# A decoder layer on one core: the next batch's context taken apart into 32 slots among the present batch's stages

## The chip, the core and the metric

The kernel runs as one program on one NeuronCore of a Trainium2 chip. The metric is the time of one execution on the device in microseconds (us), the median of several runs. All arithmetic is float32, except the attention scores, whose float32 operands are split into three bfloat16 parts.

## What is computed

For each of 8 batches: a self-attention block, a cross-attention block with an MLP, and a feed-forward block whose operands are rounded to FP4 values in blocks of 16. In short:

```python
x = x + attn(layernorm(x))               # x: (8, 512, 256), 16 heads of 16, relative keys and values
Q = layernorm(x); C = ctx                # ctx: (8, 1601, 256)
q, k, v = LN(Q) @ wq, LN(C) @ wk, LN(C) @ wv            # 16 heads of 64
out = (l2norm(q) @ l2norm(k).T) @ v @ wo                # no softmax
y = Q + out + bo
x = x + y + gelu(LN(y) @ w1 + b1) @ w2 + b2
x = x + fp4(silu(fp4(z) @ wg.T) * (fp4(z) @ wu.T)) @ wd.T       # z = layernorm(x)
```

Cross-attention has no softmax, so keys and values enter only through one matrix. With kn the normed keys and Cn the normed context, the kernel forms G = kn.T @ Cn per pair of heads, then the block diagonal of G @ wv, then M = that @ wo (1024 x 256), and needs only qn @ M for the present batch. M depends on the context alone, not on x.

## The kernel before

One hardware loop runs over the 8 batches (`Fori(0, NB)` on every engine; b is the batch). PE is TensorE, DVE is VectorE, ACT is ScalarE, POOL is GpSimd, SP issues most DMAs. The order on each engine is the order of the program text; engines meet only at semaphores, and an instruction that waits holds all that is behind it on its engine. Within a batch the stages follow one another:

1. **Projection of x.** Normed x is transposed; K, Q and V are projected; `R` (queries against the 41 relative keys) comes from four tiles of `bdk` matmuls. K and Q are split into three bfloat16 parts.
2. **Context.** 13 tiles of 128 rows of the context (the last has 65). A tile is loaded, normed (`norm_stats`, `norm_apply`), transposed (`t_ctx`), projected to 1024 key columns (`k_ctx`), squared and summed by heads, scaled by a root that POOL computes (`norm_root`, a power function, line 367), and added to G (`g_ctx`), which fills PSUM banks 0 to 3. Beside it run the transfers that prepare attention: SP stores the band part of R and the bfloat16 parts to DRAM scratch and reads the parts back, rearranged, as `Kp`, `Kfar` and `Qp`; POOL builds the far edges of the bias (`Eb`, 8 pieces of 512 KB, two buffers, line 679) in `far_edge`, and ACT's own DMA queue stores them (`store_edge`, line 832).
3. **G to M** (G is transposed, multiplied by wv, masked, multiplied by wo).
4. **Attention**, four tiles of 128 queries by 16 heads: scores on PE, bias and minimum on DVE (line 1115), exponential on ACT (line 862), transposes and the product with V on PE. SP loads bias windows and stores probabilities.
5. **Band, output projection, norm**: `transpose_band`, `weigh_band`, `combine`, `project`, layer norm.
6. **Cross-attention**: `project_q`, roots on POOL, transposes and the product with M; then the norm of y.
7. **MLP** (two products, 8 blocks of 128 hidden units).
8. **FFN**: two quantisations of 256-row halves (`quant_scale`, `quant_abs`, `quant_count`, `quant_finish`), `gate_up` and `down` for four tiles with a quantisation each. POOL's share of a tile is `quant_divide` (line 405) and `quant_finish` (lines 434 and 439). The norm of the next batch's x runs behind the last tile.

Before the loop, the FFN weights are quantised and transposed; this takes the first 124 us.

## Time and profile before

| | |
|---|---|
| median of 3 runs | 3678.69 us (3668.11 to 3689.46) |
| the profiled execution | 3670.19 us |
| its span, from the first to the last instruction | 3668.3 us |
| PE busy | 2691.3 us, 73% |
| DVE busy | 1985.8 us, 54% |
| ACT busy | 1195.6 us, 33% |
| POOL busy | 1153.9 us, 31% |
| mean granted TensorE clock | 0.897 of full speed |
| moved by DMA | 259.07 MB |

The busy shares are averages over stages with different limits, and no engine is near its whole span. The stages repeat every 440 us or so, and they are told apart by asking for the busy time in windows of one batch. The second batch, from 576.8 to 1017.2 us, is the one read below.

### The profile page before, as it was taken

How to read it: one execution, taken by the hardware profiler on the slowest of the kernel's cores; microseconds unless marked ns; L12 is line 12 of the kernel's file. 1: busy time of each engine (PE TensorE's matmuls, PEld its weight loads, DVE VectorE, ACT ScalarE, POOL GpSimd, SP SyncE). 2: the span in 40 equal slices, each digit the busy share in tenths (PEclk: the TensorE clock that was granted, in tenths of full speed). 3: DMA queues.
4: the chain of work that ended last, by engine and by line, in shares of the span. 5: the costliest groups of instructions: out<-in, count | busy, mean ns of one | idle time of the engine just before them, and what ended most of it. 6: DMA issues, size and time to landing. Idle time of an engine off the chain costs nothing.

```text
span 3668.3 us, 48646 instructions
## 1 busy us (share of the span) xinstructions
PE 2691.3 (73%) x14836; PEld 1813.0 (49%) x14884; DVE 1985.8 (54%) x4001; ACT 1195.6 (33%) x1925; POOL 1153.9 (31%) x812
## 2 busy tenths in 40 slices
PE   0487777877787776867768777687777867787776
PEld 0255544554455544555445545355544554455544
DVE  5646465463754537545375554646455464654537
ACT  1226222271233612344123432225223271233611
POOL 1352223422243123521235222362223522244122
PEclk9999988998899987998879989799888998899987
DMA  6365004650056400663008520364104650056400
GB/s 195 34 127 135 20 6 53 123 145 7 2 85 124 112 6 13 100 128 82 6 18 127 120 58 6 32 137 126 28 6 48 128 141 6 8 76 127 118 6 6
DMA packets 503886, 259.07 MB, mean 71 GB/s; under 512 B 213166, under 2 KB 501702, under 8 KB 502598
## 3 DMA queue, kind: packets, MB, share of 16 engines
q1 hardware_dynamic: 436982, 221.53, 31.0%
q10 hardware_dynamic: 66560, 33.56, 4.0%
q8 instruction: 142, 2.33, 0.2%
q14 instruction: 202, 1.65, 0.2%
HBM read 129.67 MB, written 125.35 MB: 70 GB/s over the span
## 4 chain that ended last, share of the span: by engine, by line
PE 50%; DVE 19%; issue 10%; ACT 8%; POOL 4%; DMA 4%; ACTq 1%; DVEq 1%; POOLq 0%; another core or an unknown queue 0%
PE PS L1273 44%; PE PS L1276 7%; DMA bias_scr<-M 4%; DVE arena L422 3%; ACT arena L862 2%; ACT arena L869 2%; DVE arena L427 2%; DVE arena L419 2%; POOL rn L367 1%; POOL rstd L367 1%; POOL arena L439 1%; DVE PS L1115 1%; DVE arena L424 1%; DVE arena L1072 1%; DVE arena L429 1%
## 5 line engine op out<-in xcount | busy, mean ns | idle before, releaser
L1276 PE MATMUL PS<-ident,arena 128*128 128x128 f32 (+1 forms) x3356 | 571.3, 299 | 628.5 <-POOL arena L439 289.8
L1276 PEld LDWEIGHTS PS<-ident,arena 128*128 128x128 f32 (+1 forms) x3356 | 410.9, 152 | 822.4 <-POOL arena L439 313.0
L1273 PE MATMUL PS<-arena 128*17 128x128 f32 (+5 forms) x6624 | 729.5, 318 | 106.6 <-ACT arena L869 60.1
L1273 PEld LDWEIGHTS PS<-arena 128*17 128x17 f32 (+2 forms) x6656 | 510.2, 126 | 214.1 <-ACT arena L869 68.1
L367 POOL TENSOR_TENSOR rn<-rn,mhalf 128x16 f32<-128x16 f32 (+1 forms) x136 | 412.9, 3036 | 475.0 <-DVE rn L1065 264.7
L1115 DVE CUSTOM_DVE_ANT_0 PS<-PS,arena 128x512 f32<-128x512 f32 x512 | 343.2, 712 | 97.0 <-PE PS L1273 68.9
L1273 PE MATMUL PS<-cwk,arena 128*128 128x512 f32 (+1 forms) x832 | 376.1, 595 | 23.7 <-ACT arena L801 21.0
L862 ACT ACTIVATE arena<-PS,nmax 128x512 f32<-128x512 f32 x512 | 352.1, 690 | 74.3 <-DVE nmax L1115 65.5
L716 POOL TENSOR_TENSOR arena<-arena,mass_mask 128x512 f32<-128x512 f32 x128 | 163.3, 1276 | 571.9 <-ACT arena L862 571.9
L367 POOL TENSOR_TENSOR rstd<-rstd,mhalf 128x1 f32<-128x1 f32 (+3 forms) x153 | 104.0, 680 | 719.6 <-DVE rstd L380 300.9
L1063 DVE TENSOR_REDUCE ss<-arena 128x16 f32<-128x1024 f32 (+1 forms) x104 | 126.9, 1220 | 285.1 <-ACT arena L807 285.1
L869 ACT ACTIVATE arena<-PS 128x512 f32<-128x512 f32 x384 | 228.9, 597 | 120.5 <-PE PS L1273 116.7
L801 ACT ACTIVATE arena<-PS 128x1024 f32<-128x1024 f32 (+1 forms) x104 | 106.4, 1023 | 483.0 <-PE PS L1273 473.4
L1273 PEld LDWEIGHTS PS<-cwk,arena 128*128 128x128 f32 (+1 forms) x832 | 152.7, 186 | 190.0 <-issue 180.8
L1273 PE MATMUL PS<-wdT,arena 128*128 128x256 f32 (+1 forms) x384 | 165.1, 603 | 32.1 <-ACT arena L943 32.1
L439 POOL TENSOR_TENSOR arena<-arena 128x704 f32<-128x704 f32 (+2 forms) x58 | 87.1, 1501 | 322.2 <-DVE arena L429 322.2
L1273 PE MATMUL PS<-cwq,arena 128*128 128x512 f32 x256 | 160.9, 793 | 35.1 <-DVE arena L1217 27.9
L1122 DVE COPY arena<-PS 128x512 f32<-128x512 f32 x128 | 88.4, 691 | 166.2 <-PE PS L1273 166.2
L679 POOL TENSOR_TENSOR M<-tail_mask,arena 128x1024 f32<-128x1024 f32 x64 | 122.1, 1908 | 112.7 <-DMA bias_scr<-M 112.7
L1273 PEld LDWEIGHTS PS<-wdT,arena 128*128 128x128 f32 (+1 forms) x384 | 112.0, 309 | 82.1 <-ACT arena L943 44.8
L1273 PE MATMUL PS<-M,arena 128*128 128x256 f32 x512 | 118.1, 384 | 40.2 <-issue 19.5
L1072 DVE TENSOR_TENSOR arena<-arena,rn 128x1024 f32<-128x1024 f32 (+1 forms) x104 | 126.6, 1218 | 22.9 <-POOL rn L367 22.9
(163 smaller groups left out, 3763.2 us busy)
## 6 DMA issues: line engine op xcount, KB each, us to landing
arena<-bias_scr SPq DMA_DIRECT2D x128, 336.0 KB, 3.2
prob_scr<-arena SPq DMA_DIRECT2D x128, 336.0 KB, 3.7
bias_scr<-M ACTq DMA_DIRECT2D x64, 512.0 KB, 4.8
q_scr<-arena SPq DMA_DIRECT2D x128, 128.0 KB
arena<-k_scr SPq DMA_DIRECT2D x64, 256.0 KB, 10.9
arena<-q_scr SPq DMA_DIRECT2D x128, 128.0 KB, 3.2
arena<-in_ctx SPq DMA_DIRECT2D x96, 128.0 KB, 2.5
arena<-far_scr SPq DMA_DIRECT2D x64, 182.0 KB, 17.0
```

The source lines that it names most:

```text
L367: pool.tensor_tensor(x, x, mhalf[0:x.shape[0], 0:x.shape[1]], ALU.pow).then_inc(done, 1)
L422: st(eng.scalar_tensor_tensor(c, a, m, c, ALU.is_gt, ALU.add))
L439: eng.tensor_tensor(X, qc[0:parts, p, 0:n], qh[0:parts, p, 0:n], ALU.mult).then_inc(quant_out, 1)
L679: pool.tensor_tensor(Eb[:, k, :, :], tail_mask[:].unsqueeze(1).broadcast_to([128, HC, 128]), bcast(Rb[:, t, k * HC:(k + 1) * HC, BAND], 12 ...
L716: pool.tensor_tensor(prod[:], P[:, (g % 2) * HG:(g % 2 + 1) * HG, t * 128 + BAND:t * 128 + BAND + 128], mass_mask[:].unsqueeze(1).broadcas ...
L862: act.activation(P[:, (g % 2) * HG + j, PAD:PAD + S], bank(j), ACT.Exp, bias=nmax[:, j:j + 1], scale=-1.0).then_inc(probs_ready, 1)
L869: act.activation(PTs[:, j, :], bank(TBANKS[j]), ACT.Copy).then_inc(pt_copied[0], 1)
L1063: st(dve.tensor_reduce(ss[0:n, p, :], csq[0:n].rearrange("p (h c) -> p h c", c=XD), AX.X, ALU.add))
L1072: dve.tensor_tensor(k, k, bcast(rn[0:n, q % 2, :], XD), ALU.mult).then_inc(cs_ready, cinc(i))
L1115: dve.tensor_tensor_reduce(out=bank(j), in0=bank(j), in1=Wz[:, at:at + S], scale=-0.25, scalar=BIG, op0=ALU.add, op1=ALU.min, accum_out=nm ...
L1273: return pe.matmul(o, l, r, start=start, stop=stop, **kw)
L1276: return pe.transpose(o, i, ident[0:i.shape[0], 0:i.shape[0]])
```

## The change

The context part of a batch leaves its place in the batch. For batch 0 it runs before the loop; inside the loop every engine works on the present batch b and on the context, the G-to-M products and the projection of x of batch b + 1.

- **Slots.** The context is cut into 26 half tiles (two passes of 13 tiles over 512 key columns each), run as 32 slots numbered -6 to 25, each slot with one piece on each engine. `SLOTS_AT` says behind which piece of the present batch each slot stands, the same on every engine: -6 to 2 behind the four band tiles, 3 to 6 behind the output projections, 7 to 11 behind the norm, 12 to 23 among the cross-attention tiles, 24 and 25 at the norm of y. The MLP products have none.
- **PSUM.** The present batch keeps banks 0 to 3 from the band stage to the MLP, the slots have banks 4 to 7. Banks that were double buffers in the band and cross stages become single: the band transposes (banks 0 and 1 for every tile), `project_q` (banks 2 and 3), the projected keys of a slot (bank 6).
- **G to M** of b + 1 stands between the four `second` products of the MLP; the projection of x of b + 1 follows them, ahead of the FFN.
- **The transfers that prepare attention** (`prepare`) stand, for b + 1, behind the present batch's attention on SP, in this order: R, the parts, a wait for all of them, Kp, Qp, Kfar, and then the far edges, now 16 pieces of 256 KB in two buffers, issued by SP and no longer by ACT. SP's stores of the output come after all of them.
- **POOL** builds the 16 far edges four at a time inside the FFN loop, behind each tile's `quant_divide` and the previous tile's `quant_finish`; each waits for the store of the piece before it in its buffer, and the first waits for `part2_ready`.
- At the start of an iteration SP waits until the output is stored, then loads the first bias windows.
- The loop still runs 8 times, each with the next batch's context; the ninth context is a batch of zeros appended to the input.

```diff
+PASSES = 2
+CSTEPS = PASSES * CT
+HALF = INNER // PASSES
+MP = NM // PASSES
+FIRST = -6
+MBANKS = (6, 7, 2, 3)
+LOADS = ((0, 1), (1, 4), (4, 8), (8, 12), (12, 13))
+EQ = HG * 128
+SLOTS_AT = {("band", 0): (-6, -5, -4), ("band", 1): (-3, -2), ("band", 2): (-1, 0), ("band", 3): (1, 2),
+            ("wo", 0): (3,), ("wo", 1): (4,), ("wo", 2): (5,), ("wo", 3): (6,), "ln": (7, 8, 9, 10, 11),
+            ("x", -1): (12, 13, 14), ("x", 0): (15, 16, 17), ("x", 1): (18, 19), ("x", 2): (20, 21), ("x", 3): (22, 23),
+            "yn": (24, 25), ("h", 1): (), ("h", 3): (), ("h", 5): (), ("h", 7): ()}
...
+            def prepare(nb):
+                for t in range(T):
+                    sp.wait_ge(r_act, 2 * (T * nb + t + 1) + 1)
                     sp.sem_inc(waits_alone, 1)
                     sp.dma_start(bias_scr[t].rearrange("h (p r) -> p h r", r=SKEW)[:, :, 0:BAND],
                                  Rb[:, t, :, 0:BAND]).then_inc(bias_stored, 16)
-
-                def store_keys(i):
-                    if i == 0:
-                        sp.wait_ge(part1_ready, 2 * (b + 1) + 1)
-                        sp.sem_inc(waits_alone, 1)
-                        sp.wait_ge(part2_ready, 2 * (b + 1) + 1)
-                        sp.sem_inc(waits_alone, 1)
-                        sp.wait_ge(far_ready, 3 * (b + 1) + 1)
-                        sp.sem_inc(waits_alone, 1)
+                sp.wait_ge(part1_ready, 2 * (nb + 1) + 1)
+                sp.sem_inc(waits_alone, 1)
+                sp.wait_ge(part2_ready, 2 * (nb + 1) + 1)
+                sp.sem_inc(waits_alone, 1)
+                sp.wait_ge(far_ready, 3 * (nb + 1) + 1)
+                sp.sem_inc(waits_alone, 1)
+                for i in range(PARTS):
                     sp.dma_start(k_scr[i].rearrange("(c r) s -> r c s", c=2), kparts[:, i, :, :]).then_inc(parts_stored, 16)
                     sp.dma_start(far_scr[i].rearrange("(c r) s -> r c s", c=2), farparts[:, i, :, :]).then_inc(parts_stored, 16)
-
-                def store_q(slot):
+                for slot, part in enumerate(SLOTS_Q):
                     for c in range(2):
                         sp.dma_start(q_scr[slot * HD:(slot + 1) * HD, c * HC:(c + 1) * HC, :].rearrange("d h s -> h d s"),
-                                     qparts[:, SLOTS_Q[slot], c, :]).then_inc(parts_stored, 16)
-
-                def more_ctx(i, q):
-                    if i < PARTS:
-                        store_keys(i)
-                    elif i < PARTS + 4:
-                        store_q(2 * (i - PARTS))
-                        store_q(2 * (i - PARTS) + 1)
-                    if exists(i + CSLOTS):
-                        load_ctx(i + CSLOTS)
-                ctx_unrolled(more_ctx)
-                sp.wait_ge(parts_stored, 16 * STORES * (b + 1) + 1)
+                                     qparts[:, part, c, :]).then_inc(parts_stored, 16)
+                sp.wait_ge(parts_stored, 16 * STORES * (nb + 1) + 1)
                 sp.sem_inc(waits_alone, 1)
-
-                def load_q(t, g):
-                    sp.dma_start(Qp[:, g * HG:(g + 1) * HG, :],
-                                 q_scr[:, g * HG:(g + 1) * HG, t * 128:(t + 1) * 128]).then_inc(q_loaded[g], 16)
-
                 for slot, part in enumerate(SLOTS_K):
                     sp.dma_start(Kp[slot * HD:(slot + 1) * HD, :, :], k_scr[part].rearrange("(h d) s -> d h s", d=HD))\
                         .then_inc(k_loaded, 16)
+                for g in range(NG):
+                    load_q(nb, 0, g)
                 for slot, part in enumerate(SLOTS_K):
                     sp.dma_start(Kfar[slot * HD:(slot + 1) * HD, :, :], far_scr[part].rearrange("(h d) s -> d h s", d=HD))\
                         .then_inc(k_loaded, 16)
-                for g in range(NG):
-                    load_q(0, g)
-
+                for t in range(T):
+                    for g in range(NG):
+                        sp.wait_ge(eb_ready, NG * (T * nb + t) + g + 2)
+                        sp.sem_inc(waits_alone, 1)
+                        sp.dma_start(bias_scr[t, g * HG:(g + 1) * HG].rearrange("h (p r) -> p h r", r=SKEW)[:, :, BAND:BAND + 128],
+                                     Eb[:, g % 2, :, :]).then_inc(eb_stored[g % 2], 16)
...
+                load_ctx(b + 1)
+                load_x(b + 1)
+                prepare(b + 1)
...
+            def far_edge(nb, t, g):
+                if t == 0 and g == 0:
+                    pool.wait_ge(r_act, 2 * T * (nb + 1) + 1)
+                    pool.sem_inc(waits_alone, 1)
+                    pool.wait_ge(part2_ready, 2 * (nb + 1) + 1)
+                    pool.sem_inc(waits_alone, 1)
+                pool.wait_ge(eb_stored[g % 2], 16 * (2 * (T * nb + t) + g // 2) + 1)
+                pool.sem_inc(waits_alone, 1)
+                pool.tensor_tensor(Eb[:, g % 2, :, :], tail_mask[:].unsqueeze(1).broadcast_to([128, HG, 128]),
+                                   bcast(Rb[:, t, g * HG:(g + 1) * HG, BAND], 128), ALU.mult).then_inc(eb_ready, 1)
...
-                        quant_divide(pool, gs[:, t, :], t % 2, 128, FF)
+                        quant_divide(pool, gs[:, t % 2, :], t % 2, 128, FF)
                     if t:
-                        if t >= 3:
-                            pool.wait_ge(ht_psum, T * b + t - 1)
-                            pool.sem_inc(waits_alone, 1)
-                        quant_finish(pool, st, hq[:, (t - 1) % 2, :], (t - 1) % 2, 128, FF, NQ0 + b * QPB + NXQ + t - 1)
+                        quant_finish(pool, st, qc[:, (t - 1) % 2, :], (t - 1) % 2, 128, FF, NQ0 + b * QPB + NXQ + t - 1)
+                    if t < T:
+                        for g in range(NG):
+                            far_edge(b + 1, t, g)
...
+            def slot(nb, s):
+                j = s + 3
+                if 0 <= j < CSTEPS:
+                    i, p, n = j % CT, j // CT, crows(j % CT)
+                    pe.wait_ge(ct_ready, ctile(nb, i))
+                    pe.wait_ge(kc_ready, cstep(nb, j - 1))
                     for c in range(2):
...
+                        ins = mm(bank(6, parts=n), cnT[:, i, c, 0:n], cwk[:, c, p * HALF:(p + 1) * HALF], c == 0, c == 1)
+                    ins.then_inc(ck_psum, 1)
+                i = s + 4
+                if 0 <= i < CT:
+                    n = crows(i)
+                    pe.wait_ge(caff_ready, ctile(nb, i))
+                    pe.wait_ge(ct_ready, ctile(nb, i - 1))
+                    for c in range(2):
+                        ins = tr(bank(7, c * 128, c * 128 + n), cn[0:n, i, c * 128:(c + 1) * 128])
+                    ins.then_inc(ct_psum, 1)
+                if 0 <= s < CSTEPS:
+                    i, n = s % CT, crows(s % CT)
+                    if i == 0:
+                        if s:
+                            pe.wait_ge(g_act, PASSES * nb + 2)
+                            pe.wait_ge(g_dve, PASSES * nb + 2)
+                        for k in (4, 5):
+                            mm(bank(k), zeros[:, 0:128], zeros[:], True, True, skip_group_check=True)
+                    pe.wait_ge(cs_ready, cstep(nb, s))
+                    for m in range(MP):
+                        ins = mm(bank(4 + m // 2, (m % 2) * E, (m % 2 + 1) * E), kns[0:n, s % 4, m * 128:(m + 1) * 128], cn[0:n, i, :],
+                                 False, True, skip_group_check=True)
+                    ins.then_inc(cg_done, 1)
...
+                evac_g(b + 1, 1)
+                add_x2(0)
+                copy_gt(b + 1)
+                add_x2(1)
+                mask_kv(b + 1)
+                add_x2(2)
+                copy_m(b + 1)
+                add_x2(3)
+                norm_x2(0)
+                norm_x(b + 1)
+                quant_count(dve, st, 0, 128, XQ * E, NQ0 + b * QPB)
+                norm_x2(1)
+                first_rests(b + 1)
+                quant_count(dve, st, 1, 128, XQ * E, NQ0 + b * QPB + 1)
+                second_rests(b + 1)
...
+                    if t == 0:
+                        last_parts(b + 1)
...
+                second(0)
+                transpose_g(b + 1)
+                second(1)
+                key_values(b + 1)
+                second(2)
+                context_out(b + 1)
+                second(3)
+                project_x(b + 1)
```

On DVE a slot holds, in this order: the statistics of tile s + 6, the sum of squares of step s + 2 (8 heads), the two passes that norm tile s + 5, the scaling of step s + 1. On POOL it holds the roots for the first two, on ACT the copy of the keys of step s + 3, the copy of the transposed tile s + 4 and the square of step s + 3.

## Rows read from the trace of the kernel before

**Rows 1.** Windows: length; busy PE, PEld, DVE, ACT, POOL; clock; DMA share; GB/s.

```profile
0.00:124.00 124.00, 9.10 (x42) 6.52 (x43) 82.72 (x154) 13.42 (x21) 28.14 (x27) 1.00 0.50 144
...
576.80:598.00 21.20, 14.49 (x40) 8.11 (x40) 7.82 (x18) 7.68 (x11) 2.44 (x5) 0.86 0.13 40
598.00:718.40 120.40, 102.82 (x349) 65.82 (x350) 57.11 (x103) 31.55 (x43) 62.41 (x35) 0.93 0.79 116
718.40:732.00 13.60, 9.79 (x70) 8.93 (x72) 5.43 (x9) 3.45 (x6) 3.27 (x4) 1.00 0.17 52
732.00:829.00 97.00, 68.85 (x886) 51.65 (x887) 62.25 (x162) 68.52 (x121) 20.45 (x16) 0.96 0.53 138
829.00:843.00 14.00, 13.58 (x100) 11.19 (x100) 5.68 (x18) 2.32 (x5) 0.00 (x0) 1.00 0.00 1
...
848.00:856.50 8.50, 2.50 (x8) 1.26 (x8) 6.15 (x18) 0.78 (x1) 4.86 (x6) 0.71 0.00 1
...
829.00:926.30 97.30, 75.69 (x293) 46.71 (x293) 35.32 (x78) 17.68 (x26) 23.31 (x19) 0.88 0.02 6
926.30:1017.20 90.90, 61.55 (x208) 42.73 (x208) 69.30 (x113) 17.01 (x31) 28.75 (x20) 0.79 0.02 6
...
926.30:962.10 35.80, 27.40 (x104) 20.02 (x104) 23.22 (x49) 5.00 (x8) 6.54 (x6) 0.86 0.00 1
```

**Rows 2.** PE in order of time, one tile of the context: start, length, instructions.

```profile
630.79 3.60 PE L1273 MATMUL PS<-cwk,arena 128*128 128x512 f32 x8
634.22 0.38 PE L1276 MATMUL PS<-ident,arena 128*128 128x128 f32 x2
634.44 3.62 PE L1273 MATMUL PS<-arena 128*128 128x256 f32 x16
637.90 3.60 PE L1273 MATMUL PS<-cwk,arena 128*128 128x512 f32 x8
```

**Rows 3.** DVE in order of time, one tile of the context.

```profile
636.70 1.22 DVE L1063 TENSOR_REDUCE ss<-arena 128x16 f32<-128x1024 f32 x1 [2.67 <-ACT arena L807]
...
638.04 0.48 DVE L1026 SCALAR_TENSOR_TENSOR arena<-arena,mv,rows 128x256 f32<-128x256 f32 x1
...
639.07 1.22 DVE L1072 TENSOR_TENSOR arena<-arena,rn 128x1024 f32<-128x1024 f32 x1
640.20 0.42 DVE L1015 BATCH_NORM_STATS2 bnst<-arena 128x6 f32<-128x256 f32 x1
```

**Rows 4.** SP's issues in order of time, from the context to attention.

```profile
598.15 9.93 SPq L529 DMA_DIRECT2D bias_scr<-arena  x4
...
645.83 2.44 SPq L545 DMA_DIRECT2D q_scr<-arena  x4
...
667.31 3.77 SPq L565 DMA_DIRECT2D arena<-k_scr  x8
671.13 15.54 SPq L568 DMA_DIRECT2D arena<-far_scr  x8
686.71 9.79 SPq L561 DMA_DIRECT2D arena<-q_scr  x4
```

**Rows 5.** The page, part 6: issues, KB each, median us to landing.

```profile
arena<-bias_scr SPq DMA_DIRECT2D x128, 336.0 KB, 3.2
...
bias_scr<-M ACTq DMA_DIRECT2D x64, 512.0 KB, 4.8
```

**Rows 6.** Waits, 598 to 718.4: who waited for whom, total, times, longest.

```profile
POOL M L679 <- DMA bias_scr<-M: 14.9, 2, 14.2
```

**Rows 7.** POOL and DVE in order of time, FFN tiles and the end.

```profile
978.32 1.44 POOL L405 TENSOR_TENSOR arena<-arena,qrc 128x704 f32<-128x704 f32 x1 [1.88 <-DVE qrc L397]
...
990.47 1.43 POOL L405 TENSOR_TENSOR arena<-arena,qrc 128x704 f32<-128x704 f32 x1 [1.88 <-DVE qrc L397]
...
1008.46 1.67 POOL L439 TENSOR_TENSOR arena<-arena 128x704 f32<-128x704 f32 x1 [6.10 <-DVE arena L429]
...
1016.78 0.42 DVE L1264 TENSOR_TENSOR arena<-arena,PS 128x256 f32<-128x256 f32 x1 [3.16 <-PE PS L1273]
```

931 lines of the change are left out of this document (471 added, 460 removed).

## The prediction, made before the changed kernel was run

> **What bounds the kernel now.** I read part 1 of the page first, the busy times in the table above: PE has 73% of the span and no other engine more than 54%, so nothing is full all the time and stages must be taken one by one. The windows of one batch [rows 1] give them. The reader is to see four kinds. In the context (120.4 us) PE is busy for 102.8; a full tile takes 3.60 of keys, 0.38 of transposes (partly overlapped) and 3.62 of G, one every 7.11 us [rows 2], so 13 tiles are 92.4 us of pure PE and 28 us are lost, half of it in one wait of POOL for a far-edge store, 14.9 us [rows 6]. Attention (97.0 us) mixes ACT, DVE and PE and isn't touched. From the band to the end of the first MLP product (829.0 to 926.3, 97.3 us) PE is busy for 75.7 at a granted clock of 0.88: chains of small steps on DVE, ACT and POOL. Behind it (90.9 us) DVE's quantisation sets the pace, 12.15 us a tile as POOL's steps repeat [rows 7]. DMA is heavy beside the context (share 0.79) and nearly nil from 829 to 1017 (0.02) [rows 1]: all that prepares attention hides under the context.
>
> **The gap to be won, and what is paid first.** In the loop the stages ahead of attention (21.2 + 120.4 + 13.6 = 155.2 us) leave their place. But the change runs one context pass, projection and preparation before the loop and still eight in it. So the first attention starts at:
>
> - start-up 124 [rows 1], loads of x and context behind it 3 (a 336 KB window lands in 3.2 [rows 5]);
> - 32 slots: the first three hold only norm pieces (about 2 us each), the next ten have norm pieces on DVE (3.8 each, below), nineteen are PE's 3.55: 6 + 38 + 67, and 8 of latency: 119;
> - G to M 14 [rows 1]; norm and projection of x to the last bfloat16 part 34 (the 21.2 window, 5 for the norm, 8 for R's last tiles and the parts);
> - the stores of R (four issues took 9.93 [rows 4]; 12 beyond the parts' end) and of the parts (17, below), with no work to hide them, 29; Kp, Qp and Kfar 25; 16 far edges 38; first window 4.
>
> Sum 390 us to the first bias step. The end adds no window (-4) and the launch lies 2 outside the span (3670.19 against 3668.3). So time = 388 + 8P, P being the new period, and **the kernel is only faster if P is under 410.3** ((3670.2 - 388) / 8), where a batch now takes 440.4. That bar rests on no guess about the overlap beyond the 390.
>
> **Front half, band to first MLP product (X).** Floor: PE's own work is 75.7 at clock 0.88, 66.6 at full clock, and the slots add 92.4, together 159. Slot by slot it comes out longer, since each slot also holds DVE pieces in DVE's program order: half of 1.22 for the sum, half of 1.22 for the scaling, and for the first 13 slots two of 0.48 and 0.42 plus small ones [rows 3]; with its self-waits (0.15 us steps between them) 3.7 us a full slot.
>
> - Band, now 14: nine slots. DVE 5.7 of its own, four light slots at 2.1, five full at 3.7: 33. The band transposes now have one bank, so tile t+1's wait for an ACT copy that stands behind tile t-1's slots: about 4 us at each of two tiles. 41.
> - Output projection: four slots at 3.7 and 1 to 1.5 of DVE's own each: 21.
> - Norm: five slots of PE 3.55 = 17.8, but slot 8's scaling stands behind the whole norm chain on DVE, 7 of the window's 8.5 us [rows 1]: PE stalls 5.5; transposes and copies 2.2. 25.5.
> - Cross: four `project_q` at 3.6 for eight records and four M products at 3.6 [rows 2], transposes 4.2, twelve slots (the last without keys) 41, evacuation of G at slot 13, 2. 76.
> - Norm of y 7.3 (its chain is as long as now; PE's last two slots hide under it), first MLP product 14.9 at full clock.
>
> X = 185 against 97.3. Bounds 159 (PE without a stall) and 200.
>
> **Back half, end of the first MLP product to the last output (T).** Now 90.9 [rows 1]. The first tile's quantiser scale stands at 35.8 [rows 1]. Put in front of it: G-to-M matmuls between the second MLP products, 9.8 of PE; the norm of x, 5; the projection, 21.2; and a serial piece: `quant_abs` of the second half waits on ACT behind the copies of R, and `quant_count` behind it, 7. That is 79; `last_parts`, two of 1.2 and one of 0.9, end at 82. From there:
>
> - SP stores 6 + 16 pieces. 4 of the q kind cost 2.44 to issue [rows 4], so 16 take 9.8, the keys' 3, landing 4: 17. At 99.
> - Kp, Kfar and Qp: before, their issue took from 667.3 to 696.5, 29.2 us [rows 4], with two 512 KB edge stores beside them. Alone I take 25; bounds 18 and 30. At 124.
> - Only now is the first far edge stored, since SP issues in order; 256 KB land in about 3.5 (4.8 for 512 KB, 3.2 for a 336 KB window [rows 5]). At 127.5.
> - POOL has stood since 82 + 2: the third far edge needs the first one's buffer. Behind it on POOL are `quant_divide(1)` and `quant_finish(0)`, for which ACT, DVE and PE's `down(0)` wait. DVE counts tile 0 and scales tile 1 meanwhile, then it is out of work too.
> - Then three tiles at 12.15 or, by the edges, two buffer cycles of 4.8 and 5 of POOL's own, about as much: 36.5; and from the last `quant_finish` (1008.46) to the last output (1017.2) 8.7 [rows 7].
>
> T = 127.5 + 1.5 + 36.5 + 8.7 = 174. **The stall is 36 us of it**: without it the tiles would follow from 79 on, 79 + 4 x 12.15 + 8.7, and 2 for the edges' own time, 138. Its bounds are 25 and 45.
>
> A rule of the Trainium skill bears on the edges' move from ACT's issue to SP's (page DMA: Bandwidth & Descriptors, section Issuing engines are not separate DMA queues): DMAs from any engine share 16 DMA engines, and several issuers save only issue time. Taken so, the move costs 16 issues at 0.4, 6 us over the batch, and T would be about 145. The trace agrees on the sharing (14.9 us of waiting even from ACT's own queue [rows 6]); the rest of the stall comes from program order and buffers, which the rule doesn't cover.
>
> Between iterations, now hidden under G to M: output store and the wait for it 2.5, window issue and landing 4 [rows 5]: 6.5. Attention 97.0.
>
> P = 97 + 185 + 174 + 6.5 = **462.5**, 22 more than now: all 155 us taken out come back, 88 in X, 83 in T, 6.5 between. Time = 388 + 8 x 462.5 = **4088 us**, 11% slower, set against the profiled 3670.19; the median shown lies 8.5 higher, which is within what I can't resolve.
>
> **The rivals.**
>
> 1. *No stall of POOL.* The edges land early, as when the loads drain faster than their issue shows. For it: DMA is idle when `prepare` starts, and loads have no context loads beside them. Against: SP's order. P = 426.5, time 3800.
> 2. *PE sets the front half.* DVE's and ACT's order costs nothing, X = 159 + 5. For it: once full, the context took 7.11 us a tile, no more than its own matmuls [rows 2]. Against: each slot is followed by a piece of the batch with a serial chain. P = 441.5, time 3920.
> 3. *Faster: engines, not chains, bind everywhere.* PE never idles from the band to the MLP (159), because its clock stays at full and each slot covers a wait, and the same full packing behind it leaves DVE alone: 69.3 busy now [rows 1], some 18 more for what moves there, and starts and ends, T = 120. P = 97 + 159 + 120 + 6.5 = 382.5, time 3448. It decides as soon as the two halves together lose under 28 us to waits (P under 410.3). Against: both halves have named waits of over 25.
> 4. *Worse:* a full slot costs 4.3 on DVE and the edges queue behind each other's landings (6 a cycle): X 195, T 185, P 483, 4250.
>
> **Chances.** Forecast 0.60, rival 1 0.13, rival 2 0.12, rival 3 0.08, rival 4 0.07. From no change, measurement here can tell about 0.5%. Faster 0.08, same 0.02 (between rivals 1 and 3), slower 0.90. Range: the forecast's own is 4000 to 4180 (each of X, T off by 6); taking in rivals 1 and 2, 3800 to 4190.
>
> **What would show it.** First bias step at 390; period 462; POOL idle for some 35 to 43 us in each FFN, released by a DMA of the far edges, with DVE idle in the same stretch; DMA share above 1 there; band to MLP 185 with the granted clock at 1.0 and PE idle some 14%. Wrong if the FFN shows no POOL wait over 15 us, or if the first bias step comes before 350.

## The result and the profile after

The changed kernel takes 4299.28 us (4297.52 to 4303.79), the kernel before 3676.12 on the same chip: 1.169 of its time, interval 1.166 to 1.173. Direction and mechanism came out as forecast. The size did not: 4088 was forecast, 4190 was the upper end of the range.

The page's part 1 and two groups of its part 5 (busy and mean of one, then the idle time of the engine just before them and what ended it):

```profile
PE 2823.7 (66%) x15346; PEld 1925.3 (45%) x15346; DVE 2101.9 (49%) x4415; ACT 1302.0 (30%) x2282; POOL 1351.9 (31%) x1041
...
L679 POOL TENSOR_TENSOR arena<-tail_mask,arena 128x512 f32<-128x512 f32 x144 | 177.5, 1246 | 596.6 <-DMA bias_scr<-arena 561.6
...
L404 DVE TENSOR_REDUCE am<-arena 128x44 f32<-128x704 f32 (+2 forms) x58 | 46.6, 803 | 433.4 <-POOL arena L454 420.4
```

PE, DVE and ACT are emptier than before (66, 49 and 30% for 73, 54 and 33%), POOL is at its 31%. POOL alone stands 561.6 us in front of its far-edge products, for the stores of earlier ones, and of the 433.4 us that DVE stands idle before its scalings 420.4 are for POOL's quantiser. The second batch by stages, in the columns of [rows 1]: attention; band; output projection; norm; cross attention; norm of y; first MLP product; from there to the first row tile's scaling; the row tiles:

```profile
871.10:968.60 97.50, 70.82 (x878) 53.01 (x878) 62.05 (x161) 68.30 (x120) 20.41 (x16) 0.92 0.55 138
968.60:1018.40 49.80, 40.66 (x163) 27.13 (x164) 25.78 (x76) 10.34 (x23) 13.71 (x14) 0.79 0.11 33
1018.40:1038.00 19.60, 19.35 (x82) 13.59 (x81) 15.57 (x41) 6.77 (x16) 9.63 (x9) 1.00 0.01 1
1038.00:1062.70 24.70, 20.75 (x73) 13.15 (x71) 13.47 (x37) 7.24 (x13) 12.22 (x8) 0.93 0.00 1
1062.70:1139.00 76.30, 72.78 (x270) 49.10 (x271) 32.62 (x59) 20.14 (x31) 35.07 (x20) 0.98 0.00 1
1139.00:1146.70 7.70, 5.29 (x25) 3.65 (x24) 5.44 (x14) 0.84 (x2) 4.94 (x6) 0.98 0.00 1
1146.70:1162.90 16.20, 15.51 (x32) 6.64 (x32) 0.55 (x1) 6.67 (x10) 2.17 (x4) 0.90 0.11 33
1162.90:1242.00 79.10, 58.53 (x234) 41.65 (x235) 39.34 (x75) 23.57 (x39) 12.59 (x10) 0.85 0.36 17
1242.00:1352.80 110.80, 32.78 (x96) 21.52 (x94) 48.09 (x52) 9.47 (x20) 42.02 (x32) 0.61 0.60 110
```

X is rows two to seven, 194.3 us (forecast 185), T the last two, 189.9 (174). Nearly all of X's excess is in the band: 49.8 instead of 41, at a granted clock of 0.79 (1.3 more are in the first MLP product, and the output projection gives 1.4 back). All of T's is in the last row, where PE is busy for a third of the time.

What T waits for, on POOL in order of time (batch before that one). A far edge is L679, the divide of a row tile L420:

```profile
746.91 2.13 POOL L420 TENSOR_TENSOR arena<-arena,qrc 128x704 f32<-128x704 f32 x1 [12.92 <-DVE qrc L412]
750.51 2.36 POOL L679 TENSOR_TENSOR arena<-tail_mask,arena 128x512 f32<-128x512 f32 x2 [1.46 <-DVE arena L1116]
805.71 1.05 POOL L679 TENSOR_TENSOR arena<-tail_mask,arena 128x512 f32<-128x512 f32 x1 [52.84 <-DMA bias_scr<-arena]
...
807.98 1.38 POOL L420 TENSOR_TENSOR arena<-arena,qrc 128x704 f32<-128x704 f32 x1
```

and on SP, whose issues run in program order:

```profile
754.25 10.34 SPq L553 DMA_DIRECT2D q_scr<-arena  x16
768.19 3.77 SPq L558 DMA_DIRECT2D arena<-k_scr  x8
772.00 12.90 SPq L533 DMA_DIRECT2D arena<-q_scr  x4
784.94 6.67 SPq L563 DMA_DIRECT2D arena<-far_scr  x8
791.81 16.66 SPq L569 DMA_DIRECT2D bias_scr<-arena  x4
```

The first two edges are built by 752.9 and their first store is issued at 791.8, behind 17 us of stores and 23.5 us of load issues. It lands just before 805.7, 13.9 us after its issue. The loads issued ahead of it are still landing: the eight of Kfar do so at 793.2 to 803.9, the store at 805.5. In windows from the first load's issue to that landing (the last two columns are the DMA share and GB/s):

```profile
768.00:784.00 16.00, 0.00 (x0) 0.00 (x0) 0.00 (x0) 0.00 (x0) 0.00 (x0) 0.50 1.07 113
784.00:792.00 8.00, 0.00 (x0) 0.00 (x0) 0.00 (x0) 0.00 (x0) 0.00 (x0) 0.50 1.28 139
792.00:806.00 14.00, 0.00 (x0) 0.00 (x0) 0.00 (x0) 0.00 (x0) 0.29 (x1) 0.50 1.09 123
```

For 52.84 us POOL does nothing, and from 768 us on no engine does. Every batch has one such wait (52.2 to 53.1 us), and 8 of them and the prologue's 67.3 make most of the 561.6. The DMA share above 1 is the one that the prediction gave as a sign.

The tables below give four stretches of a batch, read from the order of time and averaged over a run's eight batches (the border over seven): scores (first to last bias step), front (from there to the last sum of the cross attention), back (from there to the last output) and border (to the next first bias step).

### The profile page after: what moved, and what is told of

Read it like the earlier page. It is cut to its first block, busy times and chain, and to the rows that moved or that the text cites. A ratio compares the mean times of both kernels' runs of the same rounds, so it can differ in the third digit from the quotient of the medians.

```text
span 4301.3 us, 51796 instructions
## 1 busy us (share of the span) xinstructions
PE 2823.7 (66%) x15346; PEld 1925.3 (45%) x15346; DVE 2101.9 (49%) x4415; ACT 1302.0 (30%) x2282; POOL 1351.9 (31%) x1041
## 4 chain that ended last, share of the span: by engine, by line
PE 50%; DVE 15%; issue 9%; SPq 8%; ACT 6%; DMA 5%; POOL 3%; ACTq 1%; DVEq 0%; POOLq 0%
PE PS L1341 44%; PE PS L1344 7%; DMA bias_scr<-arena 3%; SPq L533 3%; SPq L553 2%; ACT arena L885 2%; DVE arena L442 2%; ACT arena L878 2%; SPq L563 1%; DVE arena L437 1%; POOL rstd L382 1%; DMA q_scr<-arena 1%; DVE PS L1144 1%; DVE arena L439 1%; POOL arena L454 1%
## 5 line engine op out<-in xcount | busy, mean ns | idle before, releaser
L1341 PE MATMUL PS<-arena 128*17 128x128 f32 (+6 forms) x6864 | 809.9, 320 | 140.8 <-ACT arena L878 71.1
L1341 PEld LDWEIGHTS PS<-arena 128*17 128x17 f32 (+3 forms) x6864 | 553.7, 128 | 311.5 <-issue 93.7
L1341 PE MATMUL PS<-cwk,arena 128*128 128x512 f32 (+1 forms) x936 | 476.7, 634 | 14.5 <-ACT arena L798 14.5
L382 POOL TENSOR_TENSOR crn<-crn,mhalf 128x8 f32<-128x8 f32 (+1 forms) x234 | 419.8, 1800 | 177.7 <-DVE crn L1060 176.8
L679 POOL TENSOR_TENSOR arena<-tail_mask,arena 128x512 f32<-128x512 f32 x144 | 177.5, 1246 | 596.6 <-DMA bias_scr<-arena 561.6
L793 ACT ACTIVATE arena<-PS 128x512 f32<-128x512 f32 (+1 forms) x234 | 139.7, 597 | 699.1 <-PE PS L1341 699.1
L404 DVE TENSOR_REDUCE am<-arena 128x44 f32<-128x704 f32 (+2 forms) x58 | 46.6, 803 | 433.4 <-POOL arena L454 420.4
L1058 DVE TENSOR_REDUCE css<-arena 128x8 f32<-128x512 f32 (+1 forms) x234 | 159.6, 682 | 94.1 <-ACT arena L803 92.3
L382 POOL TENSOR_TENSOR crs<-crs,mhalf 128x1 f32<-128x1 f32 (+1 forms) x117 | 69.9, 598 | 406.8 <-DVE crs L1051 398.8
L1079 DVE TENSOR_TENSOR arena<-arena,crn 128x512 f32<-128x512 f32 (+1 forms) x234 | 160.4, 685 | 74.9 <-POOL crn L382 74.0
L382 POOL TENSOR_TENSOR rn<-rn,mhalf 128x16 f32<-128x16 f32 x32 | 93.0, 2905 | 290.2 <-DVE rn L1245 290.2
```

The lines of the kernel that those rows point to most:

```text
L382: pool.tensor_tensor(x, x, mhalf[0:x.shape[0], 0:x.shape[1]], ALU.pow).then_inc(done, 1)
L679: pool.tensor_tensor(Eb[:, g % 2, :, :], tail_mask[:].unsqueeze(1).broadcast_to([128, HG, 128]), bcast(Rb[:, t, g * HG:(g + 1) * HG, BAND] ...
L793: act.activation(kns[0:n, j % 4, :], bank(6, parts=n), ACT.Copy).then_inc(kc_ready, 1)
L1058: st(dve.tensor_reduce(css[0:n, j % 2, :], csq[0:n, j % 2, :].rearrange("p (h c) -> p h c", c=XD), AX.X, ALU.add))
L1079: dve.tensor_tensor(k, k, bcast(crn[0:n, j % 2, :], XD), ALU.mult).then_inc(cs_ready, 1)
L1341: return pe.matmul(o, l, r, start=start, stop=stop, **kw)
```

## The experiments

All are edits of the changed kernel unless the text says otherwise. Where no range or interval stands beside a time, it is that of one run, good to some 0.3%.

### 1. The edges taken out of the loop, and their stores alone

POOL doesn't build the edges, and SP's stores of them go too, by the lines of the second diff:

```diff
-                    if t < T:
-                        for g in range(NG):
-                            far_edge(b + 1, t, g)
```

> Left out: the far edges of the bias are neither built nor stored for any batch but the first (16 GpSimd products and 16 stores of each next batch). Measured so far in the changed kernel: period 490.9 us, of which 189.9 from the end of the first MLP product to the last output, with one GpSimd wait of 52.8 and row tiles of 14.4 instead of 12.15. Theory A (the edges cost both, the wait for their stores and the slower tiles beside their building): the stage falls to about 126 to 130, the period to 427 to 431, the time to 3800 to 3835 us. Rival B (the wait alone goes; the tiles stay at 14.4 for another reason): period 438, time about 3885. Rival C (SyncE's serial stores and loads of the keys end the batch anyway): the period stays over 465 and the time over 4100.

For the second run the loop above stays, and SP leaves its stores out (POOL then waits for no store, and ACT waits once a batch until the edges are built):

```diff
             def prepare(nb):
...
+                if nb is not 0:
+                    return
                 for t in range(T):
                     for g in range(NG):
                         sp.wait_ge(eb_ready, NG * (T * nb + t) + g + 2)
```

> Left out: the stores of the far edges of every batch but the first; they are still built, by the same 16 GpSimd products in the same places, which wait for nothing. Against the run without any edges the difference is the price of building them beside VectorE. Theory A (GpSimd's tensor products slow VectorE and lie in the row tiles' chain): some 9 to 15 us a batch more than the run without edges, time about 3880 to 3950. Rival B (building is free, the whole loss is the wait for the stores): within 3 us a batch of it, within 25 us in all.

Measured: 3850.1 and 3899.9 us. Against 4299.3 that is 56.1 us a batch for the edges, 49.9 of it for their stores and 6.2 for the building. The first lies between its theories A and B: the tiles do speed up, but not all four. POOL's divides without edges:

```profile
1180.94 2.14 POOL L420 TENSOR_TENSOR arena<-arena,qrc 128x704 f32<-128x704 f32 x1 [12.92 <-DVE qrc L412]
1187.74 1.44 POOL L420 TENSOR_TENSOR arena<-arena,qrc 128x704 f32<-128x704 f32 x1 [4.67 <-DVE qrc L412]
...
1199.88 1.44 POOL L420 TENSOR_TENSOR arena<-arena,qrc 128x704 f32<-128x704 f32 x1 [1.88 <-DVE qrc L412]
...
1214.39 1.44 POOL L420 TENSOR_TENSOR arena<-arena,qrc 128x704 f32<-128x704 f32 x1 [4.24 <-DVE qrc L412]
```

They follow each other by 6.8, 12.14 and 14.5 us: 12.15 [rows 7] holds for the middle one, and the last waits for `gate_up(3)`, which the change put behind `down(0)`: PE starts it at 1205.7, right behind that product, and the divide follows at 1214.4. The second run falls in its theory A's time and below its 9 to 15 us a batch.

### 2. The stores in another order

With four buffers instead of two, in the room of the queries and keys; the four stores of a query tile at each of four places in SP's order:

```diff
+                store_edges(nb, 0)
                 for slot, part in enumerate(SLOTS_Q):
...
+                store_edges(nb, 1)
                 for slot, part in enumerate(SLOTS_K):
                     sp.dma_start(Kp[slot * HD:(slot + 1) * HD, :, :], ...
...
```

> Nothing left out. Four edge buffers instead of two (in the room of the queries and keys, free once their parts are taken), and SyncE issues the four edge stores of a query tile in between: tile 0 before the stores of the query parts, tile 1 before the loads of the keys, tile 2 before those of the far keys, tile 3 behind them. Theory A (the loss is the edge stores standing behind 17 us of stores and 23.5 us of loads in SyncE's queue): GpSimd hardly waits, period 438 to 450, time 3885 to 3985. Rival B (the edges' own transfers are the limit, 16 of them at 2.2 us each, wherever they stand): their 35 us are on the path at least in part, period 460 to 475, time 4065 to 4180.

Measured: 3978.6 us, 40.1 a batch better, within A's time and far from B's (the first bias step also comes 14 us earlier, 368.4 for 382.3, so the batches themselves gain 38.8). "Hardly waits" was too much: what is left is on POOL, whose last edges wait for stores that stand behind the loads of Kp and Qp:

```profile
1242.80 1.05 POOL L684 TENSOR_TENSOR arena<-tail_mask,arena 128x512 f32<-128x512 f32 x1 [10.15 <-DMA bias_scr<-arena]
```

So I went one step further: buffers in the room of the normed x, half the edges built ahead of the row tiles, all stored ahead of the loads, which wait until the stores have landed.

```diff
-        Eb = carve(2 * EQ, (2 * EQ,), ot_at)...
+        Eb = carve(NG * EQ, (NG * EQ,), 2 * PARTS * 512)...
...
                         add_bo(b + 1)
+                for t in range(2):
+                    for g in range(NG):
+                        far_edge(b + 1, t, g)
                 for t in range(T + 1):
...
```

> Nothing left out. Four edge buffers lie in the room of the normed x (free after the value projection), so that building no longer waits for the last parts of the queries and keys: GpSimd builds query tiles 0 and 1 before the first row tile of the FFN, tiles 2 and 3 behind the first two scalings, and SyncE stores them before the key loads. Known: the changed kernel's period is 490.9 us, 450.8 with the stores in between (10 us of waits for a landing left in the last row tile), 440.9 with edges built and not stored, 434.8 without edges. Theory A (once no store stands behind a load, what is left is the building, half of it in GpSimd's idle time before the first row tile): period 436 to 441, time 3855 to 3905. Rival B (16 stores of 256 KB cost their 35 us wherever they stand, now before the part stores): the loads of the keys come late instead and attention starts late, period 450 to 460, time 3970 to 4060.

Measured: 3937.6 us, 45.2 a batch better, between the two theories. The wait has moved ahead of the first divide (1185.8), for the stores of the first four edges. These stand behind no load, but behind SP's four stores of R (320 KB each), the last of which lands at 1179.2; the first edge's store is issued at 1166.4 and lands at 1180.4, 14.0 us later, as behind the loads:

```profile
1164.62 4.73 POOL L682 TENSOR_TENSOR arena<-tail_mask,arena 128x512 f32<-128x512 f32 x4
1180.58 1.05 POOL L682 TENSOR_TENSOR arena<-tail_mask,arena 128x512 f32<-128x512 f32 x1 [11.24 <-DMA bias_scr<-arena]
```

```
us a batch             scores  front  back   border
changed kernel           88.1  180.5  212.1   10.1
no edges                 89.1  180.5  157.0    7.5
edges built, unstored    88.7  180.3  164.6    6.6
stores in between        89.1  180.0  171.0   11.9
edges early              88.3  179.9  168.0   11.0
```

So the place in SP's order cost 40 to 45 us a batch, and rival B of both runs, that 16 stores cost their 35 us wherever they stand, is out. What wasn't tried is the issuer: the edges' stores back on ACT's queue, as in the kernel before. The front does not answer to the edges at all; it is the other question.

### 3. Where the context steps stand

```diff
-            ("wo", 0): (3,), ("wo", 1): (4,), ("wo", 2): (5,), ("wo", 3): (6,), "ln": (7, 8, 9, 10, 11),
+            ("wo", 0): (), ("wo", 1): (), ("wo", 2): (), ("wo", 3): (), "ln": tuple(range(-6, 26)),
...
```

> Nothing left out. All 32 context steps of the next batch stand in one place, behind the first norm, instead of being dealt out over band, output projection, norm and cross attention (and TensorE waits for all attention rows before the first output projection). Theory A (dealing them out hides the short waits of the present batch's own steps): the stretch from the band to the first MLP product grows from 194.3 to about 209, the period to 506, the time to about 4420. Rival B (TensorE is the bound of the stretch either way, the slots only fill what they take): within 4 us a batch, time 4270 to 4330. Rival C (the slots in between stall TensorE more than they fill, as the 4.25 us wait in the band shows): 5 to 10 us a batch faster, time about 4220 to 4260.

```diff
-SLOTS_AT = {("band", 0): (-6, -5, -4), ("band", 1): (-3, -2), ("band", 2): (-1, 0), ("band", 3): (1, 2),
+SLOTS_AT = {("band", 0): (), ("band", 1): (-6, -5, -4), ("band", 2): (-3, -2), ("band", 3): (-1, 0),
...
```

> Nothing left out. The first context steps of the next batch stand behind the second band tile instead of the first, the following ones one place later each, up to the norm. In the changed kernel TensorE idles 4.25 us in the band for the first normed context tile (974 us) and the granted clock is 0.5 to 0.8 for the next 25 us, where the kernel before has 1.0 in its band. Theory A (the first step comes before its tile is loaded and normed, and the band then runs at the lower clock; that is the 9 us by which the stretch from band to first MLP product was longer than forecast): the band's clock is 1.0, the stretch shortens by 4 to 9 us, time 4225 to 4270. Rival B (the idle time and the low clock only move to where the steps now start, or to the norm): within 2 us a batch, time 4280 to 4315. Rival C (fewer steps hidden in the band: 3 steps more in the norm): 2 to 5 us a batch slower, up to 4340.

```diff
-SLOTS_AT = {("band", 0): (-6, -5, -4), ("band", 1): (-3, -2), ("band", 2): (-1, 0), ("band", 3): (1, 2),
+SLOTS_AT = {("band", 0): (), ("band", 1): (), ("band", 2): (), ("band", 3): (),
...
+            "yn": (18, 19), ("h", 1): (20, 21), ("h", 3): (22, 23), ("h", 5): (24,), ("h", 7): (25,)}
```

> Nothing left out. The steps are dealt out behind the output projections, the norm, the cross attention and the MLP products (8 of the 32 among the last), none in the band. Theory A (TensorE has no gap among the MLP products, so 6 context tiles cost their full 5.4 us there, and the band runs without them at full clock): the stretch from the band to the last MLP product stays within 4 us of the changed kernel's, time 4265 to 4335. Rival B (it matters little where the steps stand as long as they are dealt out, but the band's low clock goes): 4 to 9 us a batch faster, 4225 to 4265. Rival C (the band and MLP places are worse for the waits of the present batch): 5 us a batch slower or more, over 4340.

Measured: 4408.5, 4305.0 and 4179.4 us. (In the first and the third PE also waits for all attention rows before the first output projection.) All in one place costs 13.7 us a batch (A): that is what the dealing out is worth. One tile later changes nothing (B). With none in the band and six among the MLP products (my expectations say eight; the two before them stand in the norm of y, as two did) it is **15.0 us a batch faster**, beyond all three theories I wrote.

```
us a batch             scores  front  back   border
all in one place         87.7  193.7  213.0    9.9
one tile later           88.3  179.8  212.7   10.0
none in the band         88.0  150.0  227.6    9.8
```

30.5 us less in front, 15.5 more behind (the MLP is in that stretch). Two windows of that kernel (fourth batch), the band up to DVE's last combine, and norm of y with the first MLP product:

```profile
1909.40:1925.40 16.00, 14.67 (x106) 11.78 (x104) 6.15 (x20) 3.05 (x7) 0.00 (x0) 0.96 0.34 104
...
2052.60:2089.30 36.70, 35.80 (x119) 21.59 (x119) 12.82 (x31) 13.65 (x20) 17.85 (x15) 1.00 0.05 15
```

Between the same marks the band shrinks from 44.7, with seven of its nine steps, to 16.0. Norm of y and first MLP product, with eight steps in place of two, grow from 23.3 to 36.7, by 13.4 where PE's busy time grows by 15.6 (20.2 to 35.8): a step there costs no more than its matmuls, since the first ones also fill the waits of the norm. In the band seven steps take 28.7 us for 20.8 more of PE's busy time. What part of this is a lower clock and what part waits is the next question.

### 4. The wait in the band and the clock

PE in the band of the changed kernel, second batch, and the windows just there:

```profile
971.53 1.28 PE L1341 MATMUL PS<-bdv,arena 128*128 128x68 f32 x10
977.05 0.68 PE L1344 MATMUL PS<-ident,arena 128*128 128x128 f32 x2 [4.25 <-DVE arena L1072]
978.78 1.33 PE L1344 MATMUL PS<-ident,arena 128*128 128x128 f32 x5 [1.04 <-ACT arena L909]
...
983.22 2.34 PE L1341 MATMUL PS<-bdv,arena 128*128 128x68 f32 x10
```

```profile
974.60:980.60 6.00, 2.51 (x9) 1.70 (x10) 3.77 (x14) 0.87 (x2) 2.12 (x3) 0.59 0.01 4
980.60:986.60 6.00, 6.00 (x22) 4.78 (x22) 1.17 (x5) 0.00 (x0) 0.00 (x0) 0.50 0.00 0
```

PE waits 4.25 us for the first normed context tile. Not for its load, which was issued at 967.5: on DVE the tile's first norm piece stands behind the band's own combine, which waits for PE's band products,

```profile
972.84 0.26 DVE L1189 RECIPROCAL rl<-PS 128x16 f32<-128x16 f32 x1 [2.33 <-PE PS L1341]
...
973.94 0.42 DVE L1046 BATCH_NORM_STATS2 cbn<-arena 128x6 f32<-128x256 f32 x1
...
976.44 0.48 DVE L1072 SCALAR_TENSOR_TENSOR arena<-arena,crs,rows 128x256 f32<-128x256 f32 x1 [0.16 <-DVE arena L1068]
```

so that PE's transposes of that tile wait for a chain that starts at the product PE did just before them. With the steps one tile later the same wait stands one tile later, which is why that won nothing:

```profile
985.54 0.69 PE L1344 MATMUL PS<-ident,arena 128*128 128x128 f32 x2 [4.26 <-DVE arena L1072]
```

After it the granted clock is 0.5, the lower of its two levels (1.2 of 2.4 GHz), and ten records that took 1.28 us at 971.5 take 2.34 at 983.2. Two kernels fill the wait with products of zeros, whose results nobody reads (the second diff is against the first):

```diff
                     weigh_band(t)
+                    if t == 0:
+                        for _ in range(14):
+                            mm(bank(7), zeros[:, 0:128], zeros[:], True, True, skip_group_check=True)
                     slots(("band", t))
```

> Nothing left out. In the changed kernel TensorE waits 4.25 us in the band for the first normed context tile, and the granted clock is 0.5 to 0.8 for 25 us from there on. Here 14 products of zeros (0.3 us each) stand in that place. Theory A (the low clock follows from the idle time, and the low clock is why the band took 49.8 us where 41 was forecast): the band's clock is near 1.0, 6 to 9 us a batch shorter, time 4225 to 4250. Rival B (the clock falls whatever TensorE does there, or the band is held by the waits between the engines and not by its clock): within 2 us a batch, 4285 to 4315.

```diff
-                        for _ in range(14):
-                            mm(bank(7), zeros[:, 0:128], zeros[:], True, True, skip_group_check=True)
+                        for _ in range(20):
+                            mm(bank(4), zeros[:, 0:128], zeros[:], True, True, skip_group_check=True)
                     slots(("band", t))
+                    if t < 2:
+                        for _ in range(5):
+                            mm(bank(4), zeros[:, 0:128], zeros[:], True, True, skip_group_check=True)
```

> Nothing left out. As the run with 14 products of zeros in the band's wait (4271.1 us; there 1.2 us of idle time were left and the clock fell all the same in most batches), now with 20 in that place and 5 in each of the two next waits. Theory A (the idle time decides on the clock): the clock stays at 1.0 through the band in nearly all batches, which makes the stretch from the last score to the cross attention's end 172 to 173 us instead of 180.7 in nearly all of them, time 4230 to 4245. Rival B (the two good batches were chance, the band is held by the waits between engines): 4265 to 4290.

Measured: 4271.1 us, then 4244.0. With 14 products the front is 174.1 and 172.7 in two batches, 176.7 in a third and 179 to 180 in five. With 30 it is 170.4 to 173.5 in all eight, 172.2 on average for 180.5, and the time 6.9 us a batch less. The first lies between its theories, the second in its theory A. The band up to DVE's last combine, and from there to the last sum of the output projection, in the changed kernel and in this one:

```profile
967.70:1012.40 44.70, 35.51 (x142) 23.25 (x142) 20.59 (x62) 8.04 (x18) 10.07 (x10) 0.76 0.12 38
1012.40:1034.90 22.50, 22.25 (x94) 15.71 (x93) 18.11 (x47) 8.16 (x19) 11.98 (x10) 1.00 0.00 1
```

```profile
963.10:999.40 36.30, 33.09 (x170) 20.55 (x171) 20.56 (x62) 8.00 (x17) 10.09 (x10) 0.99 0.15 46
999.40:1021.90 22.50, 22.25 (x94) 15.71 (x93) 18.11 (x47) 8.16 (x19) 11.99 (x10) 1.00 0.00 1
```

The same steps take 8.4 us less in the band when the clock stays up, and nothing less where it was up already. So of the 15.0 us a batch of experiment 3 about half is the clock, which in the band without steps is at 0.96; moving the steps is worth 8.1 us more than filling ((4244.0 - 4179.4) / 8).

### 5. Towards a kernel that is faster

Three more: the early edges and the steps without the band together (no other edit); the changed kernel with its last batch written out without a ninth context; and all of these with the first bias windows loaded ahead of the last output's store.

> Nothing left out. The early edges (3937.6 us alone) and the context steps of which 8 stand among the MLP products and none in the band (4179.4 us alone, 120 less than the changed kernel) together. Theory A (they lie in different stages and add up): 3937.6 - 120 = about 3818, within 15. Rival B (with the steps' last six behind the MLP the edges and steps meet on GpSimd and VectorE): 3850 to 3900.

```diff
-            with sp.Fori(0, NB) as b:
+            def batch(b, more):
...
-                prepare(b + 1)
+                if more:
+                    prepare(b + 1)
...
+            with sp.Fori(0, NB - 1) as b:
+                batch(b, True)
+            batch(NB - 1, False)
```

> Nothing left out. The last batch is written out behind the loop without the context steps, projections, parts, stores and edges of a ninth batch that nobody reads. In the changed kernel the last batch takes 484.5 us. Theory A (it then takes what the kernel before shows for the same stages: attention 97, band to first MLP product 97, from there 91 to the last output, 285 in all): time 4095 to 4115. Rival B (written out again, the instructions of the last batch are fetched late by every engine): 20 us or more of it are lost, over 4130.

```diff
                 for t in range(T):
+                    if more and t == T - 1:
+                        first_windows(b + 1)
                     sp.wait_ge(out_ready, T * b + t + 2)
```

> Nothing left out. Early edges, steps among the MLP products, the last batch without a ninth context, and the first two bias windows of the next batch loaded as soon as the last down product is done, ahead of the last output's store. Theory A: 3818 of the two, less 145 for the ninth batch's work (430 in its last batch against 285), less 4 to 5 us at each of 7 batch borders: 3640, range 3615 to 3670, which would be 1% below the kernel before and 2% above the kernel before with its edges first (3574.5). Rival B (the output's store waits behind the windows' 3.2 us and holds up the memsets of the probabilities, so nothing is won at the border): 3670 to 3690.

Measured: 3867.6, 4119.7 and 3711.0 us (the last 1.010 of the kernel before, 1.007 to 1.013). The ninth context is worth 179.5 us (4299.3 - 4119.7), a little less than theory A's 184 or more: the last back stretch takes 135.1 us where the kernel before takes 113.8 for that work. Most of these 21 us lie ahead of the row tiles: from the end of the second MLP product to the first `gate_up` pass 28.2 us where the kernel before takes 9.4, with PE waiting 14.1 and 11.2 us for POOL's quantiser of the two halves of x (before: 7.5, once). The change has both halves quantised and transposed ahead of the first product, and that order is still in this kernel. It wasn't tried alone, and rival B, late instructions, isn't ruled out by a run of its own. The steps' 15.0 us a batch came to 8.7 on top of the early edges. The time lies in rival B's range but not for its reason: the steps lengthen the back by the same 15.6 us with and without the early edges (168.0 to 183.6, 212.1 to 227.6). The front gains 4.5 us less than before (26.0 for 30.5): three of its eight took 160 to 163 us instead of 149, as one in eight did before; why is open. Of the miss of 71 us in the last kernel 50 are this one, of edges and steps together, and 21 are those of the last back stretch. Its border is 6.5 us instead of 12.1, a gain of 5.6 for the 4 to 5 expected.

What pays is the same observation in the **kernel before**. Its own edges have the same defect: POOL waits 14.2 us for a store that lands behind the loads of Kp and Kfar [rows 6]. That store was issued by ACT at 671.2, behind SP's eight loads of Kp, and landed at 690.8, so another issuing engine did not spare it the queue.

```diff
-        EDGES_AT = 2
+        EDGES_AT = 0
```

> Nothing left out. The kernel before with one constant changed: its far edges begin at its first context step instead of the third, so that they are built and stored two steps earlier. In the kernel before, the stores of the later edges land behind SyncE's loads of the keys too. Theory A (the same queueing that costs the changed kernel 37 to 56 us a batch also ends the context phase of the kernel before): 5 to 20 us a batch faster, time 3510 to 3635. Rival B (the context phase there is bound by TensorE, 102.8 us busy of 120.4, and the edges lie beside it): within 2 us a batch, 3655 to 3690.

Measured: **3574.5 us (3563.8 to 3583.8), 0.972 of the kernel before, interval 0.970 to 0.974**, the fastest of all. There PE stands 10.12 us before the last context tile's transposes (first row), for DVE, whose root on POOL is queued behind the waiting edge. Two steps earlier the last edge is built just as SP's loads begin, no edge comes behind it to wait, and PE's wait is gone (second row):

```profile
694.26 0.48 PE L1276 MATMUL PS<-ident,arena 65*128 65x65 f32 x2 [10.12 <-DVE arena L1032]
```

```profile
1100.09 0.28 PE L1276 MATMUL PS<-ident,arena 65*128 65x65 f32 x2
```

Last, the zeros in four waits of the kernel before (6.2, 3.5, 3.7 and 6 us), with its edges as they were and with its edges first:

```diff
                 for t in range(T):
                     project(t)
+                fill(pe, bank(3), 26)
...
                 project_q(1)
+                fill(pe, bank(0), 13)
...
+                fill(pe, bank(7), 14)
                 for t in range(T):
                     pe.wait_ge(yz_ready, T * b + t + 2)
...
+                fill(pe, bank(5), 24)
                 transpose_xq(0)
```

> Nothing left out. The kernel before with products of zeros in four waits of TensorE: 26 before the cross attention's first transpose (6.2 us idle), 13 before its third query projection (3.5), 14 before the MLP (3.7), 24 before the FFN (6). Theory A (each of these waits costs the lower clock for 10 to 12 us behind it, where products of 3.3 us take 6.7): 8 to 14 us a batch, time 3562 to 3610. Rival B (these stretches are held by VectorE's chains): within 2 us a batch, 3658 to 3690. Rival C (the fill runs over the wait): slower, over 3690.

> Nothing left out. The same four fills in the kernel before with its edges first (3574.5 us). Theory A: both gains add up, 3574 less 64 to 112, time 3462 to 3510. Rival B (VectorE's chains hold these stretches): 3558 to 3590. Rival C (the fill runs over the waits): over 3590.

Measured: 3723.1 and 3598.1 us (0.979 of the kernel before, 0.976 to 0.983): slower by 50 and by 24 than the same kernels unfilled. Both times lie in rival C's range, but the fills don't run over: behind the four of them PE still waits 0.6, 0.7, 0.7 and 2.3 us. With the edges first the mean clock did rise (0.920 against 0.899), but the front took 83.7 us for 84.4 and the back 114.7 for 113.9: DVE's and POOL's chains hold those stretches. One row of the filled kernel:

```profile
915.84 0.66 PE L1280 MATMUL PS<-ident,arena 128*128 128x128 f32 x4 [2.33 <-POOL arena L439]
```

After 5.1 us of zeros PE still waits for POOL's quantiser. Where the loss itself comes from isn't settled: with the edges as they were it is spread over the front (85.3 for 83.5), the back (115.7 for 113.8) and the context behind it (159.3 for 155.9), where nothing was filled.

## Why the prediction was right and wrong

**The frame held.** First bias step at 382.3 us (forecast 390), attention 97.5 (97), output projection 19.6 (21), norm 24.7 (25.5), cross attention 76.3 (76), norm of y 7.7 (7.3), first scaling at 79 behind the MLP (79). P was 488.9 us on average, (4299.3 - 388) / 8, for 462.5 (490.6 from first bias step to first bias step); and 8 x 26.4 is the whole miss of 211 us. X looks better term by term than it was by a little luck: the first MLP product took 16.2 for 14.9, which output projection and norm, 2.2 under together, make good; and X's terms add up to 185.7, not 185. The bar of 410.3 was nowhere near. Rival 1 (no stall, P 426.5) is what the run without edges nearly built, (3850.1 - 388) / 8 = 432.8, with the band as it is; so even without any edges, built or stored, the change loses.

**The step on the first edge's store failed ("256 KB land in about 3.5").** It took 13.9 us from issue (791.8) to POOL's start, for it queued behind the 20 loads that SP had issued just before. I had taken the landing from medians over stores that mostly have nothing before them [rows 5]; the page's median for these stores is still 3.1. The kernel before had the sign: behind its wait of 14.2 us [rows 6] stands a store that took 19.6 us to land. This is 10 us too few; SP's stores (17.1 for 17) and loads (23.5 for 25) were right, and the first edge's store was issued 3.5 us earlier than forecast (120.5 us behind the first MLP product for 124), so the stall's end came 7 us late. POOL's wait was 52.8 us for the 35 to 43 forecast, and the cost of the stores, 49.9 us a batch by experiment 1, lies outside the stall's bounds of 25 to 45.

**The step on the remaining tiles ("36.5") was short by 9.** Between the stall's end and the last output lay 55.6 us for 46.7. The divides followed by 12.1 and 14.4 us. I had taken the edges' building as hidden beside the tiles; taking it out saved 6.2 us a batch (experiment 1). The other part is `gate_up(3)` behind `down(0)`, which I saw in the diff and gave no price.

**The step on the band ("41") was wrong in its clock.** I summed it at full clock, and gave a granted clock of 1.0 from band to MLP as a sign; it was 0.79 in the band. PE's wait for the first context tile had no term, since I had counted the pieces' own durations and not the chain from PE over DVE's combine, the norm and POOL's root back to PE. The wait itself stays when it is filled; what goes is the low clock behind it, and with that 8.3 us of the front, against the 9.3 by which it was over.

**The border ("6.5") took 10.1: the loop's own return had no term.** SP, from the last output's store to the next iteration's first windows:

```profile
849.65 12.29 SPq L634 DMA_DIRECT2D out<-arena  x4
867.87 6.43 SPq L587 DMA_DIRECT2D arena<-bias_scr  x3
```

The last sum ends at 861.3; its store is issued at 861.6 and lands at 863.5 (2.2 us behind the sum). At 864.0 SP takes its branch back to the loop's start, and its next instruction comes at 867.3. That gap is 3.0 to 3.3 us at each of the seven borders. The window is issued at 867.9 and lands at 870.9. The kernel before shows such a gap too (2.5 to 2.8 us on SP), but there the context stage and not attention stands behind it.

**What I didn't price at all** was another place for the steps. That none stands among the MLP matmuls looked like a favour to a stage that PE fills (14.9 us, PE busy 15). It is the reverse: there a step costs its matmuls; in the band, where PE has gaps, it costs the band's chain and, as it turned out, the clock as well.

A rule of the Trainium skill, not weighed ahead (page SBUF — State Buffer, section SBUF: two separate sides), bears on the building's price: VectorE and GpSimd lock a shared pair of ports for a whole instruction, VectorE where it runs in a two-port mode or, against a GpSimd instruction that reads SBUF, where it has two inputs there. The rows agree; here DVE in the run without edges, first beside POOL's product of `quant_finish` (L449, 1189.1 to 1190.8), then alone:

```profile
1189.59 2.88 DVE L437 SCALAR_TENSOR_TENSOR arena<-arena 128x704 f32<-128x704 f32 x2
...
1226.71 1.82 DVE L437 SCALAR_TENSOR_TENSOR arena<-arena 128x704 f32<-128x704 f32 x2
```

A pair of the same instruction takes 2.88 us beside GpSimd and 1.82 alone, so what GpSimd builds "beside" DVE's quantiser can be paid by DVE; how the 6.2 us of the building divide between that and POOL's own time wasn't measured.

## What to carry to other kernels

Before a stage is moved out from over its DMAs, write down the order in which they are issued and what is still in flight, from any engine, in front of the first one that somebody waits for; a store that frees a buffer belongs ahead of the loads. Here one constant that put it there made the kernel before 2.8% faster, and the whole rebuilt schedule made it 17% slower. Work to be woven into another stage went best where the engine it needs was already full, since only its own instructions were paid there; in a stage of short dependent steps the pieces also cost waits and the clock behind them. And a wait of TensorE in a stage that it sets cost twice, once itself and once in the clock behind it; in a stage that another engine sets, keeping the clock up won nothing.

## What the runs showed of the hardware

- A 256 KB store that lands in 3.1 us (median) took 13.9 behind 20 loads from the same issuing engine, and 14.0 behind four stores of 320 KB (early edges). In the kernel before, a 512 KB store from ACT's queue (median 4.8) took 19.6 while SP's loads were in flight. The rule of the Trainium skill quoted in the prediction (page DMA: Bandwidth & Descriptors, section Issuing engines are not separate DMA queues) says that DMAs of every issuer run on the same 16 engines and interleave. The last row agrees; the rule has no price, and these rows give one.
- After 4.25 us of PE idle time, broken by two transposes and followed by 1.04 more, the granted clock was 0.5, and it came and went for another 20 us. With zeros in three quarters of the first wait the front stayed long in five of eight batches, with 30 products in none.
- The same pair of DVE instructions took 58% longer beside a GpSimd product (2.88 us for 1.82).
- Between SyncE's branch at the end of an iteration and its next instruction pass 3.0 to 3.3 us in the changed kernel, at each of seven borders; neither instruction waits for a semaphore.
